# Transposed attention scores in tiles of 32 rows and 64 columns, with the maxima added first, in a fused transformer layer on one core

## What is computed

```python
h = gamma * rmsnorm(x) + beta                       # per sequence, from cond
q, k, v = split(h @ W_q.T), split(h @ W_k.T), split(h @ W_v.T)   # 16 heads of 16
attn = softmax(0.25 * einsum('bnqd,bnkd->bnqk', q, k))
x = x + a_alpha * (merge(attn @ v) @ W_o.T)
x = x + f_alpha * (silu(h2 @ gate_w.T) * (h2 @ hidden_w.T) @ out_w.T + out_b)
out = layernorm(x) * weight + bias + tanh(cond @ lin_w.T + lin_b), again * weight + bias
```

## Time and profile before

| | us |
|---|---|
| median of 3 runs | 497.71 (497.28 to 498.92) |
| the profiled execution | 497.6 |
| its span on the core | 495.8 |
| granted TensorE clock, mean | 0.99 of 2.4 GHz |

### The profile page before, as it was taken

How to read it: one execution, slowest core, us unless ns; L and a number is a source line. 1 busy time by engine, 2 the same in 40 slices (tenths; PEclk the granted TensorE clock), 3 DMA queues, 4 the chain that set the end, 5 groups by cost and what they waited for, 6 DMA issues and landing times.

```text
span 495.8 us, 11725 instructions
## 1 busy us (share of the span) xinstructions
PE 474.9 (96%) x4465; PEld 399.2 (81%) x4465; DVE 376.2 (76%) x778; ACT 241.3 (49%) x355; POOL 270.9 (55%) x179
## 2 busy tenths in 40 slices
PE   7888999999999999999999999999999999999990
PEld 4666778898879888898888988888888978888890
DVE  5879676578876889778876888777895798594636
ACT  3873754256452655437462654437562466323330
POOL 3267555644477543955468544764548445526471
PEclk9999999999999999999999999999999999999996
DMA  8573086302723054500942036410834014500131
GB/s 197 154 201 108 1 216 141 55 2 49 209 73 78 1 156 98 147 1 0 250 64 88 0 102 152 115 34 0 198 87 117 0 44 129 128 1 14 30 73 56
DMA packets 36058, 44.21 MB, mean 89 GB/s; under 512 B 3136, under 2 KB 31040, under 8 KB 36032
## 3 DMA queue, kind: packets, MB, share of 16 engines
q1 hardware_dynamic: 36032, 43.85, 34.7%
HBM read 35.18 MB, written 4.47 MB: 80 GB/s over the span
## 4 chain that ended last, share of the span: by engine, by line
PE 86%; DVE 6%; POOL 3%; ACT 3%; DMA 1%; issue 1%; DVEq 0%; SPq 0%; POOLq 0%
PE banks L680 33%; PE banks L699 18%; PE banks L470 9%; PE banks L576 6%; PE banks L505 4%; PE banks L630 4%; PE banks L594 3%; PE banks L599 3%; PE banks L581 1%; PE banks L539 1%; PE banks L428 1%; PE banks L651 1%; POOL hs L1490 1%; DMA work_c<-xn 1%; POOL wout L1495 0%
## 5 line engine op out<-in xcount | busy, mean ns | idle before, releaser
L680 PE MATMUL banks<-x2s,gh 128*128 128x512 f32 x768 | 190.5, 397 | 0.0
L680 PEld LDWEIGHTS banks<-x2s,gh 128*128 128x128 f32 x768 | 140.5, 188 | 30.3 <-ACT x2s L945 0.4
L1490 POOL TENSOR_TENSOR hs<-act_t,hs 128x512 fp32r<-128x512 f32 x64 | 82.2, 1286 | 147.2 <-ACT hs L924 114.1
L699 PE MATMUL banks<-wout,hs 128*128 128x256 f32 x768 | 104.6, 286 | 0.8 <-POOL hs L1490 0.8
L699 PEld LDWEIGHTS banks<-wout,hs 128*128 128x128 f32 x768 | 97.7, 188 | 6.2 <-POOL hs L1490 1.2
L924 ACT ACTIVATE hs<-act_t 128x512 fp32r<-128x512 f32 x64 | 40.3, 630 | 87.2 <-DVE act_t L1266 81.2
L1262 DVE SCALAR_TENSOR_TENSOR act_t<-act_t,banks 128x512 f32<-128x512 f32 x64 | 43.9, 686 | 43.8 <-ACT act_t L917 43.2
L917 ACT ACTIVATE act_t<-banks 128x512 f32<-128x512 f32 x64 | 38.1, 596 | 74.4 <-PE banks L680 71.2
L470 PE MATMUL banks<-xs,wqk 128*128 128x512 f32 x192 | 47.4, 395 | 2.5 <-POOL xs L1442 1.6
L1194 DVE RECIPROCAL work_c<-banks 128x512 f32<-128x512 f32 x14 | 47.0, 3355 | 3.0 <-PE banks L594 3.0
L1266 DVE SCALAR_TENSOR_TENSOR act_t<-act_t,banks 128x512 f32<-128x512 f32 x64 | 44.0, 687 | 5.7 <-PE banks L680 2.4
(11 more groups left out here) (125 smaller groups left out, 664.9 us busy)
## 6 DMA issues: line engine op xcount, KB each, us to landing
xtok<-x_in SPq DMA_DIRECT2D x8, 512.0 KB, 5.0
work_c<-xn SPq DMA_DIRECT2D x16, 256.0 KB, 3.6
xres<-x_in SPq DMA_DIRECT2D x8, 512.0 KB, 6.6
row_aa<-rows_dram SPq DMA_DIRECT2D x16, 256.0 KB, 6.6
row_af<-rows_dram SPq DMA_DIRECT2D x16, 256.0 KB, 7.2
row_b<-rows_dram SPq DMA_DIRECT2D x16, 256.0 KB, 5.9
shift<-rows_dram SPq DMA_DIRECT2D x16, 256.0 KB, 6.0
y<-final SPq DMA_DIRECT2D x7, 512.0 KB, 3.2
```

Of the source, the lines that this page charges most:

```text
L680: last = mm(banks[:, base + part, :], gh[:, a, k, w:w + P], x2s[:, b, k, :], start=(n == 0), stop=(n == 5))
L699: last = mm(banks[:, t // 2, D * (t % 2):D * (t % 2) + D], hs[:, c % 2, b, P * t:P * t + P], wout[:, a, c, :], start=(c == 0 and a == b an ...
L1490: tt(hs[:, c % 2, 1, :], act_t[:, c % 2, :], hs[:, c % 2, 0, :].bitcast(F32), ALU.subtract)\
```

## The change

A half of the transposed scores becomes one call, `scores(g, h)`, for all eight sequences. The stationary operand is now a pair of heads (32 rows) with one parity left in (64 columns, the keys of one head), the moving operand is `qall`, q copied without masks, 64 columns (one sequence). Eight such tiles fill the array: four pairs, each with a bank of its own, by two parities, each with 64 partitions of that bank. A half takes 64 such matmuls in place of 16. The maxima are added first, in four matmuls of 512 columns in place of 16 of 128; for that `negmax` is spread out to one block of 64 columns for each sequence, and `sel` shrinks from 16 matrices to 2.

```diff
-        qpair = sb("qpair", [P, G, 2, TOK])
+        qall = sb("qall", [P, G, TOK])
-        negmax = sb("negmax", [P, 2, L], BF16)
+        negmax = sb("negmax", [P, 2, SEQ, L], BF16)
...
-        def bank_of_st(g, n):
-
-            return (4, 6, 4, 2)[n] if later(g) else 4 - 2 * (n % 2)
+        def base_of_st(g, h):
+
+            return 4 if later(g) and h == 0 else 2
...
-            def scores(g, n):
-
-                h, base = n // 2, bank_of_st(g, n)
-                if n == 0:
+            def scores(g, h):
+
+                base = base_of_st(g, h)
+                if h == 0:
                     if not later(g):
                         pe.wait_ge(selectors_ready, 1)
                     pe.wait_ge(negmax_ready, g + 1)
-                    pe.wait_ge(qpair_ready, 4 * g + 4)
+                    pe.wait_ge(qall_ready, 2 * g + 2)
                     pe.wait_ge(k_ready, 4 * g + 4)
-                elif n == 2 or not later(g):
-                    if n >= 2:
-                        pe.wait_ge(p_ready, 4 * g + n - 1)
-                elif n == 3:
-                    fed = 3 if is_last(g) else 5
-                    pe.wait_ge(h_steps, 2 * CH * (g - 1) + 2 * fed)
...
-                for i in range(4):
-                    b = 4 * (n % 2) + i
-                    for half, r in enumerate(rows):
-                        mm(region(i, half), kpar[r, h, b], qpair[r, h, :, L * b:L * b + L],
-                           start=(i == 0), stop=False)
-                for i in range(4):
-                    b = 4 * (n % 2) + i
-                    for half, r in enumerate(rows):
-                        last = mm(region(i, half), sel[r, SEQ * h + b], negmax[r, :, :],
-                                  start=False, stop=(i == 3))
+                elif later(g):
+                    pe.wait_ge(p_ready, 4 * g + 1)
+                    pe.wait_ge(h_steps, 2 * CH * (g - 1) + 2 * (3 if is_last(g) else 5))
+                else:
+                    pe.wait_ge(p_ready, 2)
+                for j in range(2):
+                    for half in range(2):
+                        r = slice(64 * half, 64 * half + 64)
+                        mm(banks[:, base + 2 * half + j, :], sel[r, h, :],
+                           negmax[r, j, :, :].rearrange("p b q -> p (b q)"), start=True, stop=False)
+                for b in range(SEQ):
+                    for pair in range(J):
+                        r = slice(32 * pair, 32 * pair + 32)
+                        for e in range(2):
+                            last = mm(banks[64 * e:64 * e + 64, base + pair, L * b:L * b + L], kpar[r, h, b, e, :],
+                                      qall[r, h, L * b:L * b + L], start=False, stop=(b == SEQ - 1))
                 last.then_inc(st_mm, 1)
...
-            def pair_q(g):
+            def copy_q(g):
...
-                    for j in range(2):
-                        nc.scalar.activation(qpair[:, h, j, :], banks[:, base + h, :], ACT.Copy,
-                                             scale=cst[:, C_PAIR + j:C_PAIR + j + 1]).then_inc(qpair_ready, 1)
+                    nc.scalar.activation(qall[:, h, :], banks[:, base + h, :], ACT.Copy).then_inc(qall_ready, 1)
...
             def exp(g, n):
-                base = bank_of_st(g, n)
-                act.wait_ge(st_mm, 4 * g + n + 1)
+
+                h = n // 2
+                base = base_of_st(g, h)
+                act.wait_ge(st_mm, 2 * g + h + 1)
...
             def negate_max(g):
                 dve.wait_ge(mt_mm, g + 1)
-                V.tensor_tensor(negmax[:, :, :], max_t.unsqueeze(1).to_broadcast([P, 2, L]),
-                                cst[:, C_NEG:C_NEG + 2].unsqueeze(2).to_broadcast([P, 2, L]), ALU.mult)\
+                V.tensor_tensor(negmax[:, :, :, :].rearrange("p j b q -> p (j b) q"),
+                                max_t.unsqueeze(1).to_broadcast([P, 2 * SEQ, L]),
+                                cst[:, C_NEG:C_NEG + 2 * SEQ].unsqueeze(2).to_broadcast([P, 2 * SEQ, L]), ALU.mult)\
                     .then_inc(negmax_ready, 1)
```

More of the change, by code:

```diff
@@ L101, in build @@
         cst = sb("cst", [P, C_END])
-        sel = sb("sel", [P, G * SEQ, P], BF16)
+        sel = sb("sel", [P, G, P], BF16)
         identb = sb("identb", [P, 64], BF16)
@@ L176, in build @@
         x0_steps, x0_hi, x0_lo = map(sem, ("x0_steps", "x0_hi", "x0_lo"))
-        qpair_ready, ld_linw = sem("qpair_ready"), sem("ld_linw")
+        qall_ready, ld_linw = sem("qall_ready"), sem("ld_linw")
         k_ready, q_ready, v_out, v_moved, v_ready, max_ready, negmax_ready, p_ready = map(
@@ L449, in transpose_x @@
                 if later(g):
-                    pe.wait_ge(p_ready, 3)
+                    pe.wait_ge(p_ready, 4)
                 steps = [(t, k) for t in range(TT) for k in range(KD)]
@@ L521, in scores_for_max @@
                         pe.wait_ge(q_ready, 4)
-                        pe.wait_ge(qpair_ready, 4)
+                        pe.wait_ge(qall_ready, 2)
                     if n >= 2:
@@ L559, in scores @@
                     pe.wait_ge(negmax_ready, g + 1)
-                    pe.wait_ge(qpair_ready, 4 * g + 4)
+                    pe.wait_ge(qall_ready, 2 * g + 2)
                     pe.wait_ge(k_ready, 4 * g + 4)
-                elif n == 2 or not later(g):
-                    if n >= 2:
-                        pe.wait_ge(p_ready, 4 * g + n - 1)
-                elif n == 3:
-                    fed = 3 if is_last(g) else 5
-                    pe.wait_ge(h_steps, 2 * CH * (g - 1) + 2 * fed)
-                rows = (slice(0, 64), slice(64, 128))
-                def region(i, half):
-                    return banks[:, base + half, 2 * L * i:2 * L * i + 2 * L]
-                for i in range(4):
-                    b = 4 * (n % 2) + i
-                    for half, r in enumerate(rows):
-                        mm(region(i, half), kpar[r, h, b], qpair[r, h, :, L * b:L * b + L],
-                           start=(i == 0), stop=False)
-                for i in range(4):
-                    b = 4 * (n % 2) + i
-                    for half, r in enumerate(rows):
-                        last = mm(region(i, half), sel[r, SEQ * h + b], negmax[r, :, :],
-                                  start=False, stop=(i == 3))
+                elif later(g):
[14 more added lines that the diff above has]
+                                      qall[r, h, L * b:L * b + L], start=False, stop=(b == SEQ - 1))
                 last.then_inc(st_mm, 1)
@@ L730, in first @@
                 scores(0, 0)
-                scores(0, 1)
                 first_sums(0, 0)
@@ L734, in first @@
                 first_sums(0, 1)
-                scores(0, 2)
+                scores(0, 1)
                 first_values(0, 1)
-                scores(0, 3)
                 for part in range(2):
@@ L761, in main @@
                 scores(g, 0)
-                scores(g, 1)
                 ffn_out(f, 2)
@@ L765, in main @@
                 attend(g, 0)
-                scores(g, 2)
-                scores(g, 3)
+                scores(g, 1)
                 ffn_out(f, 3)
@@ L931, in exp @@
                 elif n >= 2 or later(g):
-                    act.wait_ge(o_mm, 2 * g + n // 2)
-                b = 4 * (n % 2)
-                nc.scalar.activation(pt[:, b:b + 4].rearrange("p b (a j) q -> p a b (j q)", a=2),
-                                     banks[:, base:base + 2, :].rearrange("p a (b n) -> p a b n", b=4), ACT.Exp,
-                                     scale=SCALE).then_inc(p_ready, 1)
+                    act.wait_ge(o_mm, 2 * g + h)
+                if later(g):
+                    j = (0, 2, 2, 0)[n]
+                    dst, src = pt[:, :, j:j + 2, :], banks[:, base + j:base + j + 2, :]
+                else:
+                    b = 4 * (n % 2)
+                    dst, src = pt[:, b:b + 4, :, :], banks[:, base:base + J, L * b:L * b + 4 * L]
+                nc.scalar.activation(dst.rearrange("p b j q -> p j b q"), src.rearrange("p j (b q) -> p j b q", q=L),
+                                     ACT.Exp, scale=SCALE).then_inc(p_ready, 1)
             def o_split(g, h):
@@ L1168, in q_out @@
                     if h:
-                        dve.wait_ge(qpair_ready, 4 * g + 2)
+                        dve.wait_ge(qall_ready, 2 * g + 1)
                     for e in range(2):
```

14 lines of the change are left out of this document (7 added, 7 removed).

## The result

The changed kernel is slower: 520.42 us median (516.96 to 522.59), where before stood at 497.72 on the same chip, a ratio of 1.044 (95% interval 1.041 to 1.047). The prediction was 495.2 with a range up to 503.5, so even its widest end was missed. The profiled execution took 520.71 us.

The account below looks back on a forecast made before the run. The prediction took PE, busy 96% of the span and 86% of the chain, as the bound. Terms -2.5 (groups 2 to 6), -1.3 (group 1), +1.1 (group 7), +0.2 (group 0) sum to -2.5: 495.2 us, range 493.8 to 503.5.

Parts of the forecast that it names:

- Where PE is the bound: Whole kernel: PE is busy 96% of the span, so its time counts nearly one for one unless a wait takes it back.
- -2.5 for groups 2 to 6: Five loop iterations: shorter halves give up 1.88 us each, new waits leave a gain of 0.5 each.
- -1.3 for group 1: Group 1: PE doesn't wait for `feed` and resumes at 85.62 against 86.95, a gain of 1.3 us.
- The half at 1.55: Each half of the scores: adding 0.44, scores 1.00, tile change 0.10, taken as 1.55 us against 2.49 before.
- again 16 rounds: 1.00: Scores of a half: 128 records in 16 rounds of eight tiles take 1.00 us, like `attend`'s 16 rounds of four.
- four loads in 0.13 us: Issue pace: a round's four loads in `attend` fit into 0.13 us, so about 7 ns an instruction, 56 ns for eight.
- The first rival: Scores of a half: issue at 15.6 ns a record makes the half 2.55 us, sum +7.1, 504.8 us; chance 0.13.
- the prediction's own slope: Half's duration against the total: 0.1 us of the half moves about one microsecond in all.
- the second rival: Scores of a half: column tiles load in turn, half 2.2 us, sum +3.6, 501.3 us; chance 0.09.
- DVE's negated maxima: DVE, each group: 0.29 grows to 1.233 us, 0.94 more; in the loop it fills a hold-up, 0.1 charged to `feed(f, 4)`.
- The loop's new wait and the exponentials: Groups 2 to 6: second half waits 0.8 us for `feed(f, 4)`, then PE 0.55 for exponentials; gain 0.5 an iteration.
- Groups 7 and 0: Outside the loop: the negated maxima come 0.94 us later; group 7 loses 1.1 us, group 0 0.2.

Follow-up runs that it names:

- experiment 2: The changed kernel with SP's two bulk loads in group 1 held back until attend of group 1 is done; 517.38 us, ratio 1.038.
- experiment 9: The changed kernel with a short warm-up of PE behind group 0's transposes and the bulk loads of groups 0 and 1 held back; 520.19 us, ratio 1.044.
- 3: The changed kernel with tiles of 32 rows and 128 columns, 32 matmuls a half, in groups 0, 1 and 7 only; 511.17 us, ratio 1.025.
- 4: The wide kernel: the changed kernel with tiles of 32 rows and 128 columns, 32 matmuls a half, in all groups; 512.35 us, ratio 1.028.
- experiment 7: The changed kernel with a short warm-up, matmuls on data already there, behind the transposes of the maxima of group 0; 520.87 us, ratio 1.046.
- experiment 10: The changed kernel with the first half's tiles in groups 2 to 6 split into two of 32 moving columns, twice the instructions; 528.97 us, one run.
- the maxima first in split calls: The kernel before with the added maxima alone, old tiles, each call's exponential behind its own call; 500.32 us, with a warm-up in group 0 496.89.

## Why the prediction was wrong, point by point

- **Where PE is the bound.** Right for the loop; for groups 0, 1 and 7 it was taken for granted that PE always has its instructions. The first step that failed is this omission: the change part by part has no term for the supply of instructions, though every half grows from 96 instructions of PE to 264 (an fp32 matmul is two loads and two matmuls). The four gaps are 12.7 us. Moving other DMAs shortens the largest from 6.49 to 2.27 (experiment 2) and takes group 0's of 5.86 down to 0.92 (experiment 9); halving the instructions of the scores, together with wider tiles, takes group 1's away (3 and 4) and with it all but 0.7 of that group's 8.3 us. Bulk loads are only part of it: the gap in group 7 and the rest of group 1's came with idle or nearly idle DMA engines. Part by part the forecast was -2.5 for groups 2 to 6, -1.3 for group 1, +1.1 for group 7 and +0.2 for group 0; measured are +2.5, +8.3, +4.3 (with the end) and +8.2.
- **The clock.** The prediction had PE's durations at full clock throughout. Behind the gaps of 3.69 and 6.49, behind the wait of 1.38 and in group 7 it stood at 0.50; behind the 1.55 in group 2 it stayed at 1.00. I can't add the two costs up: experiment 7 shows that they overlap, since a faster PE only waits longer for the same fetch.
- **The half at 1.55.** Mis-sized: 2.06. The adding part was 0.54 with the change of tiles (reckoned 0.54), the scores 1.52 instead of 1.00. The step that failed is "again 16 rounds: 1.00", with its support that four loads in 0.13 us show the pace. In group 4's first half the first 32 records, four rounds, mostly follow each other at 58 ns a round; the other 96 need 1.2 us, about 12.5 ns each, 100 a round on average (experiment 10 has the loads' starts). A burst of four could not show a steady pace. The first rival had the mechanism, and too slow a pace (15.6 ns). That the instructions set it is what experiment 10 and the loads' starts show. By the prediction's own slope, one microsecond in all for 0.1 of the half, 2.06 would have brought about +2.6 and 500.3, inside its range: the other 20 us are supply and clock, which it left out.
  The Trainium skill ("TensorE: Matmul & The Clock Gate", section "Part 3: Packing small matmuls — row/col tiling") gives about 4 ns of issue for each further tile and a reordering window of 64 instructions. The trace's burst, 32 matmul records and their 32 loads, is of that length; neither the 6.8 ns between the loads of its rounds nor the 12.5 behind it is the 4 ns.
- **The column tiles** of a row group did load side by side (rounds of 55 to 72 ns), so the second rival was rightly held unlikely. The Trainium skill's statement in the same section that only a different row group overlaps is not borne out.
- **DVE's negated maxima:** right, 1.23 us, hidden in the loop behind POOL's hold-up; in group 0 the wait grew by 0.93 (0.45 to 1.38).
- **The loop's new wait and the exponentials:** right in place and mechanism. The wait ends at T + 11.80, and `gate_hidden(f, 5)` waits 0.59 for ACT (reckoned 0.55). With the half at 2.06 the prediction's own steps give a gain of zero: 11.79 + 2.06 + 0.1 + 1.92 + 0.05 = T + 15.92, what it was before. Measured is T + 16.21, since the second half took 2.13, ACT began 0.2 behind it and PE 0.13 behind ACT. The experiments give the price of the joined half: with nearly the same duration (2.48 and 2.49) the wide kernel is 0.7 a group behind before, while the maxima first in split calls (2.32) are 0.3 ahead.
- **Groups 7 and 0:** the waits for `pt` of 1.17 and 1.16 in group 7 are of the kind that was reckoned at +1.1; what is more, up to 4.3, is the gap of 0.97 and the low clock behind it (the 12 records of L675 at 442.30 take 4.61, where they took 3.05 before, at 420.74). What remains of group 0 in experiment 9, 4.8 us over before, wasn't taken apart further.

Splitting the joined half's exponentials by sequences, so that the first overlaps the rest of the scores, wasn't tried on the chip: PE would write a bank while ACT reads it.

## What to carry to other kernels

Count PE's instructions beside its busy time when matmuls are cut into more and smaller tiles: a rate that four neighbouring records show is that of a burst, and a longer run of the same shape is the row to price from. Straight code has to be fetched, a loop's body wasn't again after its first pass; a half with hundreds of instructions in straight code can stand still for 1 to 2.5 us, and for longer while bulk loads fill the DMA engines. Where one result is joined out of two calls, ask what had started between them; and where PE waits over a microsecond, fill the wait and look at the clock behind it.

## What the runs showed of the hardware

- In group 1 an instruction fetch started late under full DMA engines (share 0.94 to 1.12); with the loads held the gap fell from 6.49 to 2.27 us. In all runs, where PE stood still without a releaser it went on 2.3 to 3.0 us after the start of a packet, with idle DMA engines too (2.5 in group 7). The packets are 16 KB (0.38 MB in 23), and none came in the loop for 249 us.
- Small fp32 tiles of 32 x 64 follow each other at 58 ns for eight at first and at 100 ns on average after 32 matmul records, since every fourth round takes 134 to 200 ns and most others 55 to 72; halving their moving columns doesn't speed them up (13.5 ns a record).
- The granted clock fell to 0.50 behind a wait of 1.38 us in group 0, and also behind 84 one-column matmuls at a PE that was busy throughout; after 1.42 us of full matmuls in the same wait it didn't fall. It stayed at 1.00 behind a gap of 1.55 us (changed kernel, group 2) and one of 2.27 (experiment 2), so the length of a wait doesn't tell alone.
